# Three condition-matrix loads move to GpSimd, the first weights all go out by SyncE, and the order of the absolute values changes

## The reference

```python
W = L0_cond_weights[itok]                       # (32, 64, 64)
y = einsum('bct,bcd->bdt', x, W)                # x: (32, 64, 1024) float32
scale   = mean(abs(w), axis=0)                  # per column of L0_ffn_w
ternary = where(abs(w) < 0.05, 0, sign(w)) * scale
x = x + (y @ ternary + b)
W = L1_cond_weights[itok]
y = einsum('bct,bcd->bdt', x, W)
w = NF4_LEVELS[q_weight] * q_scale              # per group of 64, (out, in)
x = x + (y @ w.T + bias + 4 * (y @ A.T) @ B.T)
```

## Time and profile before

| | us |
|---|---|
| median of 3 runs | 360.85 |
| lowest, highest | 360.42, 361.82 |
| the profiled execution, its own time | 360.83 |
| its span, first to last instruction | 359.0 |
| busy in the span: TensorE matmuls | 352.2 |
| VectorE | 242.0 |
| GpSimd | 224.7 |
| ScalarE | 161.1 |

### The profile page before, as it was taken

The page is one execution under the profiler, slowest core; times in us unless marked ns, Lnnn a source line. Parts: engine busy times, 40 slices in busy tenths (PEclk is TensorE's granted clock), DMA queues, the critical chain, the costliest instruction groups (busy, mean ns, idle before and its releaser), DMA issues.

```text
span 359.0 us, 5496 instructions
## 1 busy us (share of the span) xinstructions
PE 352.2 (98%) x1832; PEld 298.7 (83%) x1832; DVE 242.0 (67%) x363; ACT 161.1 (45%) x285; POOL 224.7 (63%) x146
## 2 busy tenths in 40 slices
PE   8899999999999999999999999999999999999996
PEld 8768788888888888888888888888888888888884
DVE  5789969896996899873899979355262452634523
ACT  2787467776886877752232314213041130321300
POOL 0488999986976888876520220866366663666632
PEclk9999999999999999999999999999999999999999
DMA  6894411953345245333311330304215032150202
GB/s 235 289 328 138 151 31 30 339 203 115 134 168 181 88 156 203 125 120 121 108 76 62 123 118 3 120 0 155 88 63 181 1 140 103 60 182 2 117 31 88
DMA packets 27838, 44.63 MB, mean 124 GB/s; under 512 B 8834, under 2 KB 17026, under 8 KB 27810
## 3 DMA queue, kind: packets, MB, share of 16 engines
q1 hardware_dynamic: 26242, 43.67, 35.0%
q10 hardware_dynamic: 1568, 0.61, 0.7%
HBM read 27.49 MB, written 16.78 MB: 123 GB/s over the span
## 4 chain that ended last, share of the span: by engine, by line
PE 87%; DVE 3%; POOL 2%; issue 2%; ACT 2%; SPq 1%; DMA 1%; POOLq 0%; DVEq 0%; ACTq 0%
PE acc L1157 33%; PE acc L1195 32%; PE xT L1121 10%; PE acc L1137 6%; PE spare L1121 3%; POOL col_scale L596 2%; PE acc L1222 2%; DMA w_in<-in_L_ffn_w 1%; PE acc L1224 1%; DVE hl L872 1%; PE xT L1204 1%; DVE W L925 1%; ACT hh L684 0%; SPq L428 0%; SPq L426 0%
## 5 line engine op out<-in xcount | busy, mean ns | idle before, releaser
L569 POOL TENSOR_TENSOR X<-X,bias 128x1024 f32<-128x1024 f32 x28 | 67.5, 2412 | 29.3 <-PE xT L1121 29.1
L1157 PE MATMUL acc<-T,hh 128*128 128x512 f32 x192 | 76.0, 396 | 0.0
L1157 PE MATMUL acc<-T,hl 128*128 128x512 f32 x192 | 75.0, 391 | 0.0
L723 ACT ACTIVATE spare<-q_raw 128x512 f32<-128x512 int32 x96 | 56.0, 598 | 19.1 <-DVE side_p L913 5.1
L1195 PE MATMUL acc<-W,hh 128*128 128x512 f32 x192 | 61.1, 389 | 0.0
L1021 DVE TENSOR_TENSOR X<-X,acc 128x512 f32<-128x512 f32 x36 | 24.8, 688 | 34.8 <-PE acc L1195 18.6
L1121 PEld LDWEIGHTS xT<-mix,X 128*128 128x128 f32 x352 | 42.7, 192 | 1.5
L1121 PE MATMUL xT<-mix,X 128*128 128x128 f32 x352 | 42.8, 275 | 0.0
L1195 PEld LDWEIGHTS acc<-W,hh 128*128 128x128 f32 x192 | 36.0, 188 | 7.5
L1157 PEld LDWEIGHTS acc<-T,hl 128*128 128x128 f32 x192 | 36.1, 188 | 7.4
L628 POOL TENSOR_TENSOR X<-X,ys 128x512 f32<-128x512 f32 x18 | 22.6, 1286 | 31.1 <-DVE ys L1010 31.1
(11 more groups left out here) (98 smaller groups left out, 662.0 us busy)
## 6 DMA issues: line engine op xcount, KB each, us to landing
out<-X SPq DMA_DIRECT2D x26, 512.0 KB, 3.0
X<-out SPq DMA_DIRECT2D x16, 512.0 KB, 3.4
X<-in_x SPq DMA_DIRECT2D x12, 512.0 KB, 3.4
q_raw<-in_L_ffn_q_weight SPq DMA_DIRECT2D x16, 256.0 KB, 3.0
w_in<-in_L_ffn_w SPq DMA_DIRECT2D x14, 256.0 KB, 6.5
x_first<-in_x SPq DMA_DIRECT2D x4, 512.0 KB, 4.6
out<-x_first SPq DMA_DIRECT2D x4, 512.0 KB, 6.8
out<-X SPq DMA_DIRECT2D x4, 256.0 KB, 2.0
```

The lines of the kernel that those rows point to most:

```text
L569: pool.tensor_tensor(x_of(g), x_of(g), (bias1 if g >= NT else bias)[:, :], ALU.add).then_inc(s_xb, 1)
L723: act.activation(dst, q_raw[:, d % QS, :, :].rearrange("p o i -> p (o i)"), ACT.Copy, scale=slope, bias=offset).then_inc(s_line, 1)
L1157: mm = pe.matmul(acc[:, bank_of(q), :], a[:, k, :], b, start=(k == 0 and j == 0), stop=(k == KB - 1 and j == len(terms) - 1))
```

## The change

It does five things: `load_condition` takes a semaphore of its own for three loads; GpSimd issues condition 2 (first half) and both halves of condition 3, after waiting for the tokens and the zeroed `mix`; SyncE issues weights 0 to 4 in order, with x2 right behind condition 0; ScalarE issues no weight; ScalarE and VectorE take some blocks in another order, and `ABS[0]` follows. TensorE waits for the new semaphores before tiles 2 and 3.

```diff
@@ -152,7 +152,7 @@
     BOTH = ((0, 1, 4, 6), (2, 4, 6))
     SIGNED = tuple(tuple(k for k in range(KB) if k not in both) for both in BOTH)
 
-    ABS = ((2, 3, 0, 1, 5, 4, 7, 6), (0, 1, 3, 2, 5, 4, 7, 6))
+    ABS = ((2, 3, 0, 5, 1, 7, 4, 6), (0, 1, 3, 2, 5, 4, 7, 6))
 
 
     B11, B21, B22, B12, T1, T2, T3, T4 = range(8)
@@ -333,6 +333,8 @@
         s_left = [sem(f"s_left{k}") for k in range(XS)]
         s_win = [sem(f"s_win{i}") for i in range(NH * KB)]
         s_mix = [sem(f"s_mix{k}") for k in range(NM)]
+
+        s_mixp = [sem("s_mixp2"), sem("s_mixp3")]
         s_b0 = sem("s_b0")
         s_b1 = sem("s_b1")
         s_scales = sem("s_scales")
@@ -420,14 +422,14 @@
 
             return NTK * p + a + 1
 
-        def load_condition(eng, g, s):
+        def load_condition(eng, g, s, signal=None):
 
             table = mix1 if g >= NT else mix0
             c = eng.value_load(tok[0:1, 2 * (g % NT) + s:2 * (g % NT) + s + 1],
                                min_val=0, max_val=NCOND - 1)
             eng.dma_start(mix[s * C:(s + 1) * C, g % NM, s * C:(s + 1) * C],
                           table[bass.ds(c, 1)].rearrange("a c d -> c (a d)")
-                          ).then_inc(s_mix[g % NM], 16)
+                          ).then_inc(signal or s_mix[g % NM], 16)
 
         def load_weights(eng, k, n):
 
@@ -487,15 +489,11 @@
             sp.wait_ge(s_tok, 16)
             sp.wait_ge(s_fill, 1)
             load_condition(sp, 0, 0)
+            load_x(2)
             load_condition(sp, 1, 0)
-            load_x(2)
-            load_condition(sp, 2, 0)
-            load_weights(sp, 1, 0)
-            load_weights(sp, 3, 0)
-            load_condition(sp, 3, 0)
-            load_weights(sp, 4, 0)
+            for k in range(5):
+                load_weights(sp, k, 0)
             load_x(3)
-            load_condition(sp, 3, 1)
             load_weights(sp, 5, 0)
             load_weights(sp, 6, 0)
             load_weights(sp, 7, 0)
@@ -631,6 +629,11 @@
             pool.wait_ge(s_zero, 1)
             pool.affine_select(out=ident[:, :], in_=ident[:, :], compare_op=ALU.not_equal, fill=1.0,
                                base=0, pattern=[[-1, P]], channel_multiplier=1).then_inc(s_ident, 1)
+            pool.wait_ge(s_tok, 16)
+            pool.wait_ge(s_fill, 1)
+            load_condition(pool, 2, 0, s_mixp[0])
+            load_condition(pool, 3, 0, s_mixp[1])
+            load_condition(pool, 3, 1, s_mixp[1])
             sums(0, 1, KB)
             sums(1, 1, KB)
             add_bias(0)
@@ -791,9 +794,7 @@
             act.wait_ge(s_tok, 16)
             act.wait_ge(s_fill, 1)
             load_condition(act, 0, 1)
-            load_weights(act, 0, 0)
             load_condition(act, 1, 1)
-            load_weights(act, 2, 0)
             load_condition(act, 2, 1)
             high_x(0, 0)
             high_x(0, 1)
@@ -804,16 +805,16 @@
             high_x(1, 0)
             high_x(1, 1)
             absolute(0, 0)
-            absolute(0, 1)
+            signs(0, 5)
+            absolute(0, 5)
             high_x(2, 0)
             high_x(2, 1)
-            signs(0, 5)
-            absolute(0, 5)
-            absolute(0, 4)
+            absolute(0, 1)
             signs(0, 7)
             absolute(0, 7)
             high_x(3, 0)
             high_x(3, 1)
+            absolute(0, 4)
             absolute(0, 6)
             act.dma_start(b_raw[:, :, :], lora_b_v).then_inc(s_bin, 16)
             signs(1, 0)
@@ -1023,17 +1024,15 @@
             for where, value in ((mix[:, :, :], 0.0), (b_wide[:, :, :], 0.0), (ones[:, :], 1.0),
                                  (a_raw, 0.0)):
                 dve.memset(where, value).then_inc(s_fill, 1)
-            ternary(0, 0)
             low_x(0, 0)
             low_x(0, 1)
-            ternary(0, 1)
-            ternary(0, 2)
-            ternary(0, 3)
+            for k in range(4):
+                ternary(0, k)
             low_x(1, 0)
             low_x(1, 1)
             ternary(0, 4)
+            ternary(0, 5)
             low_x(2, 0)
-            ternary(0, 5)
             low_x(2, 1)
             ternary(0, 6)
             ternary(0, 7)
@@ -1103,7 +1102,12 @@
         @block.tensor
         def _(pe):
             def mixed(g):
-                pe.wait_ge(s_mix[g % NM], 32 * (g // NM + 1))
+                loaded = 32 * (g // NM + 1) - (0, 0, 16, 32)[g % NM]
+                need(pe, s_mix[g % NM], loaded)
+                if g == 2:
+                    pe.wait_ge(s_mixp[0], 16)
+                elif g == 3:
+                    pe.wait_ge(s_mixp[1], 32)
                 arrived(pe, g)
                 if g == 2 or g == 3:
                     pe.wait_ge(s_hl, NH * (g - 1))
```

## The result

| | before | after |
|---|---|---|
| median of 22 runs each | 360.80 us | 361.73 us |
| lowest, highest | 360.42, 361.82 | 360.93, 362.67 |
| the profiled execution | 360.83 us | 361.38 us |
| its span | 359.0 us | 359.6 us |

The ratio of after to before is 1.0025, with a 95% interval of 1.0017 to 1.0033: the changed kernel is 0.9 us slower. That is within the 0.5% called "the same", and inside the range, but 0.3 us had been forecast as gained, and the interval leaves out no change: the kernel moved the other way. The interval is 0.0008 to each side, so these runs tell apart much less than the 0.5% that I had allowed.

A forecast was written before the change was run, and what follows sets the result against it. TensorE was taken to bound the kernel from 24 us, with GpSimd's additions setting the column-sum matmul before that. Block 1 done 0.3 us earlier, other terms at nothing: 360.83 - 0.3 = 360.5 us, range 359.8 to 361.9.

The forecast's parts named there:

- the landings: First weight loads: weight 2 lands between 10.3 and 11.05, weight 0 from 8.8 to 9.55; early ends taken.
- the hole of 6 to 8 us: DMA engines moved 220 GB/s against 348 next, 0.26 MB short, worth 0.75 us; x2 issued 1.3 us earlier can fill it.
- bytes ahead fix a landing: First transfers: the sixth is now weight 2 with the same bytes ahead, so it lands at 11.05 at the latest.
- the forecast of the first addition: GpSimd's first addition of absolute values starts at 13.6 instead of 13.89.
- the turns between queues: DMA engines alternate between queues with work; speaks against moving weights 0 and 2, could cost over 2 us, set aside.
- the two ends: Start and end of the execution: only 1.83 us around the span was noted, with no change forecast there.
- the `ys` wait: TensorE's later wait of 0.2 us for VectorE's `ys`, whose work of 24 to 40 us sets that point.
- The 0.7 us for a matrix ahead of mixing x2: TensorE's 0.71 us wait until 10.68 for half of matrix 2 goes; mixing starts 10.0 to 10.1, no gain at the end.
- Given back: VectorE's work of 24 to 40 us doesn't move up, so the 0.3 us is waited at `ys`: 360.8; chance 0.24.
- Weight 5 late: Weight 5 still lands at 16.1, making GpSimd's third addition 0.9 us late: 361.4; chance 0.19.
- GpSimd's DMAs slow: GpSimd's matrices delay mixing x2 or its additions; 362.6 where the bound is passed; chance 0.10, of it 0.06 beyond.
- All waits gone: Additions don't bind, so TensorE's 3.5 us of waits in the first 24 us could go: 357.3; chance 0.03.

The follow-up runs named there:

- The run of the route alone: Kernel before with only its three condition matrices (2 first half, 3 both halves) issued by GpSimd, everything else in the old order; ratio 1.0013.
- the kernels with weight 1 ahead of x2: Kernel before with block 0's absolute value early and weight 1 issued by SyncE ahead of x2, without and with GpSimd issuing three matrices; 0.9993 and 0.9994.
- the run with the early absolute value: Kernel before with ScalarE taking block 0's absolute value right behind the high halves of x0, and GpSimd's sum order adapted; ratio 0.9991.
- the run of computing alone: Kernel before with only the order on VectorE and ScalarE and of the sums changed, every issue as before; ratio 1.0006.
- The kernel with the route and the early absolute value: Kernel before with GpSimd issuing three condition matrices and block 0's absolute value early, weight 1 behind x2 as before; ratio 1.0017.
- the variant with the route, the early absolute value and weight 1 ahead of x2: Kernel before with GpSimd issuing three condition matrices, block 0's absolute value early and weight 1 ahead of x2; ratio 0.9994.

## Why the prediction was right or wrong

**The step that failed: the landings.** "The sixth is now weight 2, with the same bytes ahead. The latest it lands is therefore 11.05", and weight 0 from 8.8 to 9.55. In the repeat of the changed kernel weight 2 landed at 11.64 and weight 0 at 9.87 (10.20 by the chain of the first profile), 0.6 and 0.3 us past the latest bounds; both values I took were the early ends, 1.34 and 1.07 us too early. The first addition came 0.56 (repeat) to 0.8 us late, the matmul likewise (24.19 and 24.40 for 23.6). Two thoughts were wrong in it. That x2 issued earlier would fill the hole of 6 to 8 us: it did in part (270 for 220 GB/s), and the next stretch lost more. And that bytes ahead fix a landing whichever queue they stand on: weight 0 on ScalarE's queue brings both weights back in time for the forecast of the first addition, with 0.3 MB more by 12 us or, without GpSimd's DMAs, with no more bytes at all, while the same weight as early on SyncE's queue does not. What I had set aside, the turns between queues in the Trainium skill ("DMA: Bandwidth & Descriptors", section "Queues, rings and completion order"), had the right sign; by that rule weight 0 loses its own turns on the move, and the runs agree (1.0025 and 1.0011 with it on SyncE, 0.9999 with it on ScalarE). It alone would not say that weights 1 and 2 also come later when weight 0 leads SyncE's queue, as it was measured.

**A term put at nothing: the two ends.** GpSimd's issues themselves were hidden, as forecast: 0.69, 0.52 and 0.52 us, landed some 3.5 us later, with 7.93 idle us behind them. But each of the 11 profiles with GpSimd DMAs issues its first DMA at 0.88 us of the span instead of 0.75, and has 3.32 to 3.56 us of it from the start of VectorE's last instruction on; the 8 without (before among them) have 3.14 to 3.21. The span alone overstates this, because in the same kernels less time lies around the span. In the execution's own time the ends are:

| profiles | the ends |
|---|---|
| 8 without GpSimd's DMAs | 4.95 to 4.97 us |
| 5 with them, weights 0 and 2 on ScalarE's queue | 4.85 to 4.93 |
| 6 with them, weight 0, 2 or both on SyncE's (the changed kernel and its repeat: 5.24 and 5.17) | 5.16 to 5.24 |

With the 0.13 us at the start, the route costs at most 0.1 us in the five, and 0.3 to 0.4 us in the six. So it is not a price of GpSimd's DMAs as such. It is not one of the weights' move as such either: the two runs with all weights on SyncE's queue and no GpSimd DMA have 4.96 and 4.97. Both together pay it, and no run shows why. I had bounded only what lies between the ends. The run of the route alone has ends of 4.85; its profiled 0.2 us over before are the start and the late weight 1. The kernel with weight 0 on ScalarE shows the two terms next to each other: VectorE's last instruction starts at 355.37, 0.49 earlier than before, the ends are 360.57 - 355.37 = 5.20 for 4.97, and over all runs the time is the same, 0.9999.

**The sum again.** The forecast was 360.53 with the matmul at 23.6. The matmul is 0.80 us later (0.13 of it from the start), the vanished `ys` wait takes 0.23 off, and the ends add 0.27: 361.37, and the profiled execution had 361.38. For the repeat it is 0.59, 0.23 and 0.20: 361.09, and it had 361.10. The median of the first set of runs, 361.73, lies 0.35 above its profiled execution, and that of the repeat is 361.11; the term that differs between the two sets was not found.

**Right.** GpSimd's additions set the column-sum matmul in every profile but the two of the kernels with weight 1 ahead of x2, and run 1.43 apart without holes in the changed kernel. TensorE waits 0.89 there (0.9 forecast). The 0.7 us for a matrix ahead of mixing x2 went, and gained nothing at the end. It came back one tile earlier, though: matrix 1 goes out behind x2, and mixing x1 waited 0.98, which I had not followed although the issue at 5.1 was in the text; the timeline of the run with weight 0 on ScalarE has 0.92 at the same place and still meets the forecast, so it costs nothing at the end.

**The rivals.** *Given back* did not occur: the `ys` wait vanished. It exists (0.5 in the run with the early absolute value), but behind a matmul moved the other way. *Weight 5 late* did not occur in the changed kernel; it is real where weight 5 is issued late (a wait of 0.76 in the run of computing alone, 1.05 in the changed kernel without GpSimd's DMAs). *GpSimd's DMAs slow* did not occur, and in the changed kernel mixing x2 did not wait; the price at the ends is on a side that this rival did not have. *All waits gone* did not occur. No rival held "the first weights land late", and that was the case that happened; the chance of slower by over 0.5%, 0.06, was not touched.

**A better version?** None that is shown. The smallest ratios are 0.9991 (0.9979 to 1.0002, early absolute value) and 0.9991 (0.9981 to 1.0001, weights 0 and 2 on ScalarE); both intervals include no change. The changed kernel with weight 0 on ScalarE's queue costs nothing against before and is the steadiest of all (0.44 us from lowest to highest).

**Left open.** Why weight 0 on ScalarE's queue lets the weights behind it land sooner was not tried by itself: the transfers have other neighbours in each variant, and neither the bytes moved nor the time of issue explains it alone. Nor is the price at the ends taken apart: a kernel with a single GpSimd DMA was not run.

## What to carry to other kernels

Moving a transfer to another queue is not neutral because the bytes ahead are the same: here the first weight had to stay on a queue other than the one with x2 and the next weights. Where landings decide, run the two placements against each other, since single profiles of one order of issues differed by 1.0 us in a landing. When a term lies at the kernel's two ends, read it from the execution's own time and not from the span, which showed a price for the route where the execution had nearly none. And a gain of 0.3 us on a chain is smaller than the scatter of the landings that it rests on.

## What was not expected of the hardware

**Engines that are busy with fewer bytes.** From 8 to 10 us the DMA engines' share was 0.95 at 314 GB/s with weight 0 on ScalarE, and 0.96 at 240 GB/s with it ahead of x2 on SyncE. A full share did not mean full throughput.

**The clock after a wait.** Where TensorE stood 2.10 and 2.37 us before mixing x2, the mean granted clock was 0.64 and 0.58 from 14 to 18 us. That mean is made of both levels: in the second of these it was 1.00 (2.4 GHz) up to 13 us and 0.50 (1.2 GHz) from 14 to 17. In the changed kernel, whose longest wait for a matrix was 0.98, it was 1.00. But the length of this one wait does not decide. The kernel with the route and the early absolute value stood 2.03 us at the same place, and in its profile the clock stayed at 1.00:

```profile
12.78 1.86 PEld L1129 LDWEIGHTS xT<-mix,x_first 128*128 128x128 f32 x16 [2.03 <-DMA mix<-in_L_cond_weights]
```

The changed kernel without GpSimd's DMAs did not wait before mixing x2 at all, but stood 1.21, 0.92 and 0.86 us at ternary tiles from 12.88 to 15.26, and had 0.68 from 14 to 18. Whole executions show it too: in the variant with the route, the early absolute value and weight 1 ahead of x2, those at a clock of 0.995 took 362.42 and 362.58 us, the others at most 360.82. So the wait for a matrix before x2, worth nothing by the sum, may cost some 2 us in some executions once it is long. That idle time causes the drop is read from these profiles, and no run varied it alone.
